# Moving the tie slots to GpSimd, the quarter sums to TensorE and half of the gap sums to VectorE, with scores and products issued earlier at both ends

## The reference, cut to what matters

```python
q = (x @ Wq.T).reshape(b, n, 2, HEADS, DIM_KEY).transpose(2, 0, 1, 3, 4)
sim = jnp.einsum('pbnhd,hkpd->pbnhk', q, keys)       # 2 x 8 vectors of 32 scores a token
sx, ix = jax.lax.top_k(sim[0], TOPK)                 # 16 best of each
sy, iy = jax.lax.top_k(sim[1], TOPK)
all_scores = (sx[..., :, None] + sy[..., None, :]).reshape(b, n, HEADS, TOPK * TOPK)
scores, pk_indices = jax.lax.top_k(all_scores, TOPK) # 16 best sums of pairs, and their places
wd = W_down[pk_indices]; wu = W_up[pk_indices]
h = gelu(jnp.einsum('bnd,bnhkd->bnhk', x, wd)) * jax.nn.softmax(scores, axis=-1)
return jnp.einsum('bnhk,bnhkd->bnd', h, wu)
```

## Time and profile before

| | |
|---|---|
| Median of 3 runs | 279.29 us (279.06 to 279.59) |
| Profiled execution, its own time | 281.1 us |
| Its span, first to last instruction | 279.4 us |
| VectorE busy | 259.9 us, 93% |
| ScalarE busy | 235.6 us, 84% |
| TensorE busy | 237.8 us, 85% |
| GpSimd busy | 226.0 us, 81% |
| Mean granted TensorE clock | 0.982 |

### The profile page before, as it was taken

The page is one execution under the profiler, slowest core; times in us unless marked ns, Lnnn a source line. Parts: engine busy times, 40 slices in busy tenths (PEclk is TensorE's granted clock), DMA queues, the critical chain, the costliest instruction groups (busy, mean ns, idle before and its releaser), DMA issues.

```text
span 279.4 us, 7039 instructions
## 1 busy us (share of the span) xinstructions
PE 237.8 (85%) x1562; PEld 176.8 (63%) x1562; DVE 259.9 (93%) x1715; ACT 235.6 (84%) x1048; POOL 226.0 (81%) x344
## 2 busy tenths in 40 slices
PE   7899689797889888978898889888988898879891
PEld 7456243575577667766776577657765776568690
DVE  5899999969999999999999999999999999995885
ACT  2554766868989999899999999999999999996853
POOL 7889701447688899989898989898989898989672
PEclk9999999979999999999999999999999999997997
DMA  7920000000000000010001000100010001000102
GB/s 179 279 74 1 2 0 0 2 1 0 5 0 0 5 0 1 13 31 0 2 3 40 1 0 5 39 0 5 0 39 4 1 0 41 1 1 4 38 1 77
DMA packets 11228, 6.23 MB, mean 22 GB/s; under 512 B 1457, under 2 KB 10674, under 8 KB 11186
## 3 DMA queue, kind: packets, MB, share of 16 engines
q1 hardware_dynamic: 9858, 5.12, 6.9%
q10 hardware_dynamic: 1328, 0.66, 1.1%
HBM read 3.67 MB, written 2.10 MB: 21 GB/s over the span
## 4 chain that ended last, share of the span: by engine, by line
PE 32%; ACT 32%; POOL 19%; issue 13%; DVE 3%; POOLq 0%; ACTq 0%; DVEq 0%
ACT prob L837 6%; PE scratch L1640 4%; PE sim L1548 4%; ACT p_win L936 3%; POOL past L485 3%; POOL squareT L500 3%; ACT gap L759 3%; PE t_bank L1566 3%; ACT away L971 3%; PE s_bank L1742 3%; PE s_bank L1736 2%; ACT spare L856 2%; PE s_bank L1531 2%; ACT sideT L747 2%; ACT side L729 2%
## 5 line engine op out<-in xcount | busy, mean ns | idle before, releaser
L1194 DVE MAX8 top<-rest 128x8 f32<-128x40 f32 x512 | 57.2, 184 | 0.1
L1144 DVE MAX8 top<-sim 128x8 f32<-128x32 f32 x496 | 54.0, 181 | 2.0 <-PE sim L1548 1.9
L837 ACT ACTIVATE prob<-drop 128x50 f32<-128x50 f32 x224 | 51.5, 255 | 0.0
L837 ACT ACTIVATION_READ_ACCUMULATOR prob<-drop 128x1 f32 x224 | 47.1, 212 | 0.0
L500 POOL TENSOR_TENSOR squareT<-sideT 100x512 bf16<-100x512 bf16 x31 | 32.3, 1041 | 6.7 <-ACT sideT L747 6.6
L513 POOL TENSOR_TENSOR wgt<-prob,rden 128x400 f32<-128x400 f32 x30 | 25.7, 855 | 11.8 <-DVE rden L1136 11.7
L1548 PE MATMUL sim<-sim_w,xT_all 128*128 128x512 f32 x64 | 34.7, 625 | 0.5 <-ACT xT_all L784 0.5
L485 POOL TENSOR_TENSOR past<-gap,last 128x400 f32<-128x400 f32 x31 | 26.8, 863 | 9.8 <-DVE last L1218 9.8
L507 POOL TENSOR_TENSOR drop<-gap,out_by 128x400 f32<-128x400 f32 x30 | 31.0, 1033 | 1.1 <-ACT out_by L736 1.1
L1566 PE MATMUL t_bank<-gaps_of,topT 128*128 128x200 f32 x128 | 29.2, 352 | 1.7 <-ACT topT L752 1.7
L1218 DVE MAX8 last<-slot_gap 128x8 f32<-128x22 f32 x256 | 24.4, 168 | 1.1
(11 more groups left out here) (295 smaller groups left out, 753.1 us busy)
## 6 DMA issues: line engine op xcount, KB each, us to landing
out<-y_sb SPq DMA_DIRECT2D x7, 256.0 KB, 2.3
x_sb<-in_L_attn_hidden_states SPq DMA_DIRECT2D x2, 256.0 KB, 4.0
fwq_sb<-in_L_ffn_Wq ACTq DMA_DIRECT2D x2, 256.0 KB, 5.8
x_sb<-in_L_attn_hidden_states SPq DMA_DIRECT2D x1, 512.0 KB, 5.4
wc_sb<-in_L_attn_Wc SPq DMA_DIRECT2D x1, 256.0 KB
out<-last_y SPq DMA_DIRECT2D x2, 128.0 KB, 1.9
wo_in<-in_L_attn_Wo SPq DMA_DIRECT2D x1, 192.0 KB
keys_sb<-in_L_ffn_keys ACTq DMA_DIRECT2D x1, 128.0 KB, 3.4
```

The source lines that it names most:

```text
L837: last = nc.scalar.activation(prob[d][:, h, :], drop[:, h, :], ACT.Exp, scale=-1.0, accum_out=den[d][:, h:h + 1])
L1144: last = nc.vector.max(top[n % 3][:, v, 0:8], sim_bank[n % 2][:, bass.ts(v, KEYS)])
L1194: last = nc.vector.max(top[n % 3][:, v, 8:16], rest[:, v, :])
```

## The change

1. **Tie slots.** In turns 4 to 31 GpSimd makes the spare slots: new `ties_of(n)`, three dependent instructions on 128 x 128 elements, right behind `past_of(n-2)`. It waits for `sum_above(n)`, which goes first in VectorE's turn and writes a tile `counts` instead of the score bank. `next_8(n)` waits for `ties_done`. `sim_used` is now said by `strike_above`. Tiles 0 to 3 keep VectorE's two instructions.
2. **Quarters.** `add_quarters` is gone; `expert_weights` adds the four heads in PSUM with two products instead of one transpose. `wgt4` has two buffers.
3. **Gaps.** For tiles 3, 4, 7, 8, ... 27, 28 (14 tiles) ScalarE's `out_by_of` and GpSimd's `drop_of` are replaced by VectorE's `keep_gaps`, one instruction that reads `f_bank` and `gap`, in the turns with j = 2 and 3. `transpose_sides` of the next tile waits for it.
4. **The start.** The token masks are transposed before `count_places(0)`, the block product of row 0 before the sides of tile 1, `scores(5)` before the pairs, and row 0's window scores before turn 4 instead of in it. `mark_above(3)` goes ahead of a gate reciprocal.
5. **The last row.** Row 7's block product moves from turn 31 to turn 30, in the place of the windows' value projection, which goes behind turn 31. In turn 31 `next_8(31)` isn't split; TensorE's `top_columns(31)`, `pair_gaps(31)` and `block_scores(7)` and ScalarE's `take_topT(31)` and `take_gaps(31)` are in the turn instead of behind it; GpSimd's `past_of(30)` goes ahead of L598, and L604 behind `drop_of(29)`. `late_gelu` goes ahead of `maxima(7)`.

```diff
+        def kept_by_vector(n):
+            return TB - 1 <= n < TILES - 3 and n % TB in (0, TB - 1)
...
             def drop_of(n):
-                pool.wait_ge(out_by_done, n + 1)
+                if kept_by_vector(n):
+                    return
+                pool.wait_ge(out_by_done, out_bys_until(n))
...
-            def add_quarters(n):
-                pool.wait_ge(wgt4_done, n + 1)
-                nc.gpsimd.tensor_tensor(wgt2[n % 2][:, :, :], wgt4[:, 0:2, :], wgt4[:, 2:4, :],
-                                        ALU.add).then_inc(wgt2_done, 1)
...
+            def ties_of(n):
+                pool.wait_ge(summed_above, n + 1)
+                pool.wait_ge(top_done, 2 * n)
+                nc.gpsimd.tensor_tensor(tie[:, :, :], counts[:, :].unsqueeze(2).to_broadcast([P, VECS, 8]),
+                                        tie_rank[:, :].unsqueeze(1).to_broadcast([P, VECS, 8]),
+                                        ALU.subtract).then_inc(tie_step, 1)
+                pool.wait_ge(tie_step, 2 * (n - TB) + 1)
+                nc.gpsimd.tensor_scalar(tie_off[:, :, :], tie[:, :, :], SPILL, 0.0, ALU.mult, ALU.min
+                                        ).then_inc(tie_step, 1)
+                pool.wait_ge(tie_step, 2 * (n - TB) + 2)
+                nc.gpsimd.tensor_tensor(rest[:, :, KEYS:KEYS + 8], tie_off[:, :, :],
+                                        top[n % 3][:, :, 7:8].to_broadcast([P, VECS, 8]),
+                                        ALU.add).then_inc(ties_done, 1)
...
                 if j == 0:
                     past_of(n - 2)
+                    ties_of(n)
                     drop_of(n - 3)
                     weigh(n - 4)
                     add_halves(n - 4)
-                    add_quarters(n - 4)
                     square_of(n - 2)
...
-                                               ALU.mult, ALU.add).then_inc(struck, 1)
+                                               ALU.mult, ALU.add).then_inc(sim_used, 1)
             def sum_above(n):
-                dve.wait_ge(struck, n + 1)
-                nc.vector.tensor_reduce(sim_bank[n % 2][:, 0:TIES], above[:, :, :], AX_X, ALU.add
-                                        ).then_inc(summed_above, 1)
+                dve.wait_ge(above_done, n + 1)
+                if n >= 1:
+                    dve.wait_ge(ties_done, n)
+                nc.vector.tensor_reduce(counts[:, :], above[:, :, :], AX_X, ALU.add).then_inc(summed_above, 1)
...
             def next_8(n, h):
                 dve.wait_ge(sim_used, n + 1)
+                dve.wait_ge(ties_done, n + 1)
...
+            def keep_gaps(n):
+                dve.wait_ge(count_ready, n + 1)
+                dve.wait_ge(gap_out, n + 1)
+                dve.wait_ge(prob_done, n)
+                nc.vector.scalar_tensor_tensor(drop[:, :, :].rearrange("p h c -> p (h c)"),
+                                               f_bank[:, 0:HEADS * CANDS], OUT_SCALE,
+                                               gap[n % 4][:, :, :].rearrange("p h c -> p (h c)"),
+                                               ALU.mult, ALU.max).then_inc(drop_done, 1)
...
             def turn(n):
                 b, j = divmod(n, TB)
+                sum_above(n)
                 strike_above(n)
                 if n + 1 in tiles:
                     first_8(n + 1, [0])
-                sum_above(n)
                 if j == 0:
                     maxima(b - 1)
                 invert_sums(n - 4)
-                spill_above(n)
+                if kept_by_vector(n - 3):
+                    keep_gaps(n - 3)
                 if n + 1 in tiles:
                     first_8(n + 1, [1])
-                put_ties(n)
-                if n + 1 in tiles:
                     mark_above(n + 1)
                 next_8(n, 0)
+                if n == TILES - 1:
+                    next_8(n, 1)
                 gaps_of_pairs(n - 1)
...
-                if n < TILES - TB:
-                    pe.wait_ge(wgt2_done, n + 1)
-                    last = nc.tensor.transpose(o, wgt2[n % 2][:, :, :].rearrange("p h c -> p (h c)"), ident[:, :])
+                if n <= TILES - TB:
+                    pe.wait_ge(wgt4_done, n + 1)
+                    w, heads = wgt4[n % 2], HEADS // 2
...
+                    project_pairs(b)
+                    expert_weights(n - 4)
+                    top_columns(n)
+                    window_scores(b)
+                    pair_gaps(n)
+                    block_scores(b)
                     count_places(n - 2)
...
             pair_gaps(2)
-            count_places(0)
             transpose_masks()
             project_window(0, U_VW, wv_sb)
+            count_places(0)
             count_ranks()
+            project_blocks(0, range(RATIO))
             transpose_sides(1)
-            project_blocks(0)
             project_selected(0)
+            scores(5)
+            project_pairs(0)
             count_places(1)
-            project_pairs(0)
-            scores(5)
+            window_scores(0)
```

More of the change, by code:

```diff
@@ L235, in program @@
         wgt = [sb(f"wgt{i}", [P, HEADS, CANDS]) for i in range(2)]
-        wgt4 = sb("wgt4", [P, HEADS // 2, CANDS])
-        wgt2 = [sb(f"wgt2_{i}", [P, 2, CANDS]) for i in range(2)]
+        wgt4 = [sb(f"wgt4_{i}", [P, HEADS // 2, CANDS]) for i in range(2)]
         last_drop = [sb(f"last_drop{i}", [P, HEADS, CANDS]) for i in range(2)]
@@ L334, in summed, with out_bys_until @@
             return n >= TILES - 4
+        def kept_by_vector(n):
+            return TB - 1 <= n < TILES - 3 and n % TB in (0, TB - 1)
+        def out_bys_until(n):
+            return sum(not kept_by_vector(m) for m in range(n + 1))
         def sums_until(n):
@@ L623, in turn @@
                     add_halves(n - 4)
-                    add_quarters(n - 4)
                     square_of(n - 2)
                 elif j == 2:
+                    past_of(n - 2)
+                    ties_of(n)
                     if b >= 2:
                         gate_silu(b - 2)
-                    past_of(n - 2)
                     weigh(n - 4)
@@ L643, in turn @@
                     square_of(n - 2)
-                    add_quarters(n - 4)
-                    if b >= 2 and n < TILES - 1:
+                    if b >= 2:
                         add_input(b - 2)
+                else:
+                    past_of(n - 2)
+                    ties_of(n)
+                    weigh(n - 4)
+                    add_halves(n - 4)
+                    drop_of(n - 3)
+                    square_of(n - 2)
+                    past_of(n - 1)
+                    gate_attention(b - 2)
             count_matrix()
@@ L659, in _ @@
                 turn(n)
-            past_of(TILES - 2)
+            drop_of(TILES - 3)
             add_input(B - 3)
-            drop_of(TILES - 3)
             square_of(TILES - 2)
@@ L1783, in turn @@
                     pair_gaps(n - 1)
-                    project_window(b, U_VW, wv_sb)
+                    if b < B - 1:
+                        project_window(b, U_VW, wv_sb)
+                    else:
+                        project_blocks(b, range(RATIO))
                     if n + 2 in tiles:
@@ L1788, in turn @@
                     count_places(n - 2)
+                elif n < TILES - 1:
+                    top_columns(n - 1)
+                    project_selected(b)
+                    pair_gaps(n - 1)
+                    transpose_sides(n - 2)
+                    project_blocks(b, range(RATIO))
+                    scores(n + 2)
+                    project_pairs(b)
+                    count_places(n - 2)
+                    expert_weights(n - 4)
                 else:
```

123 lines of the change are left out of this document (67 added, 56 removed).

## The result

The changed kernel takes 292.85 us (median of 4 runs, 292.08 to 294.96), the kernel before 279.44 in the same session (279.06 to 279.95). The ratio is 1.047, 95% interval 1.0435 to 1.0512: 4.7% slower, where 278.0 was predicted and the range ended at 281.8. The medians are 13.4 us apart; the profiled executions span 290.3 and 279.4 us, 10.9 apart.

The account below looks back on a forecast made before the run. The prediction took the steady part as a balance in which GpSimd becomes the bound. Start -2.85, five steady rows +2.4 and tail -0.85 gave -1.3 us: 278.0 us from 279.29, range 274.8 to 281.8.

Parts of the forecast that it names:

- The start: Turns 4 to 8: waits in turn 4 vanish, turn 5 starts 2.0 us sooner, `next_8(9)` 2.85 us sooner.
- rival 3: Start: it gives nothing lasting, as ScalarE or slow TensorE products hold the gain; 279.3 us, no change; chance 0.14.
- TensorE gets four more products ...; hidden: TensorE, steady rows: four more products of some 0.3 us, hidden as it has 24.61 of 28.17 us busy.
- the forecast's 28.65: Steady row: GpSimd's summed work of 28.65 us becomes the bound, against 28.17 now, +0.48 a row.
- The price of the ties: GpSimd's three `ties_of` instructions: 1.37 us a turn, bounds 1.31 and 1.57; 5.48 for four turns.
- rival 1: GpSimd's `ties_of` from turn 8: small instructions cost more than their size says, 1.57 a turn, 282.4 us; chance 0.28.
- GpSimd's sum without waits: GpSimd, steady row: its 1.30 us of waits go, since factors are always there, leaving only its work, 28.65.
- a loop through ScalarE and TensorE that I have left out: Sign against the forecast: GpSimd waiting for another engine in a steady row longer than 28.8 us.
- Who waits for the ties: `next_8`, and VectorE's turn behind it, waits about 1 us for GpSimd once a row, with j = 1 alone.
- The tail: Last row and after: maxima at about 258.0 instead of 258.96, last exponentials about 1.3 us sooner; gives 0.85 us.

Follow-up runs that it names:

- e11: e6 with the quarters on GpSimd again, leaving only the orders of start and tail; 278.04 us, 0.9918 of the kernel before.
- e6: The changed kernel with all tie slots back on VectorE in the score bank (PSUM) and without `keep_gaps`; 280.41 us, 1.0015 of the kernel before.
- e5: The changed kernel with all tie slots back on VectorE in the score bank (PSUM), `keep_gaps` staying; 281.50 us, 1.0057 of the kernel before.
- e2: The changed kernel without the middle of GpSimd's three tie instructions, a step left out of the result; 282.16 us, 1.0098 of the kernel before.
- e9: The changed kernel with TensorE's `expert_weights` and `count_places` moved behind the first half of `attention_out`; 288.15 us, 1.0303 of the kernel before.
- e10: e6 with the tie slots of the turns with j = 1 on GpSimd; 288.66 us, 1.0300 of the kernel before.
- e1: The changed kernel with all tie slots back on VectorE, their tiles still in SBUF; 305.79 us, 1.0859 of the kernel before.
- e13: e6 with the tie slots of the turns with j = 2 on GpSimd; 283.91 us, 1.0154 of the kernel before.
- e15: The changed kernel with the middle tie instruction as a product with a constant 0, comparison left out of the result; 289.17 us, 1.0320 of the kernel before.
- e8: The changed kernel with the middle tie instruction's two scalars from an SBUF column instead of immediates; 299.25 us, 1.0648 of the kernel before.

## Why the prediction was wrong

- **The start**: right in what moves, not in what it is worth. The maxima of turn 4 came 2.67 sooner, `sim` was no wait, and turn 5 begins at 66.41 in e11 for 68.58, 2.17 sooner (2.0 forecast). But the sum took its holes, 1.86 and 0.67 in turn 4 and 3.11 before the last maxima, from an execution whose clock had fallen just there. It also set its span (279.4) equal to the median of others (279.29), where its own time was 281.1. The forecast went on to 2.85 by `next_8(9)`; the changed kernel had 1.08 left at turn 8's maxima. The runs place part of the difference: e11 has 2.02 there (first maxima at 88.59), e6, which differs by the quarters, 1.33 (89.28). By its sign (turn 5 no sooner than 67.5) rival 3 is out, and e11 shows that the orders gain something that lasts: 1.5 to 1.9 at like clocks, start and tail together, where 2.85 + 0.85 = 3.7 was forecast. That products run slowly in turn 4, which rival 3 names, is what the clock row shows.
- **"TensorE gets four more products ...; hidden"**: the step that failed quietly. TensorE's 24.61 of 28.17 busy was no cover, since those of the turn with j = 1 (0.44 us for 0.11) lie in the one stretch that the loop runs through. 0.43 a row, 28.61 against 28.18 (e6, e11). It doesn't show in the changed kernel's sum, because there GpSimd is longer, but rows of 28.57 to 28.64 (e5, e6, e2) are what is left when GpSimd is relieved and the quarters stay: in e2 cheaper ties brought the row to the forecast's 28.65 and no further.
- **The price of the ties**: mis-sized, 1.37 taken, 1.60 measured (0.40, 0.64 and 0.42 with their gaps), just above the upper bound of 1.57. It was L463 where L472 with 0.536 was the safer neighbour. +0.92 a row. This is rival 1, and alone it would have given about 282 to 283.
- **GpSimd's sum without waits**: the step that failed most. The other terms of 28.65 were right: 28.65 + 0.92 = 29.57, and e9's row, in which GpSimd waits for nothing, is 29.61. But in the changed kernel the row is 29.57 + 0.87 of wait = 30.44, measured 30.47. The prediction had costed the ties as work on one engine, and named "a loop through ScalarE and TensorE that I have left out" as what would prove it wrong. The loop is what happened: the ties stand ahead of the halves, the halves hold TensorE's queue, and the queue holds `sideT`. The wait that the earlier trace rows show there before, 0.24 for `sideT`, was its sign, and I read it as slack.
- **Who waits for the ties**: right. `next_8` waits for them 0.43 us in the turn with j = 1 alone (1 us forecast). The larger waits of VectorE in a row, 1.45 for its maxima and 1.02 for `slot_gap`, are the loop's.
- **The tail**: right as an order, wrong in this kernel. In e11 the last row is 26.04 against 27.44 before, 1.40 shorter (0.85 forecast for the whole tail), but the 27.44 have a clock fall in them, which cost about 1.5 us in the long row of e10; so the gain of this order isn't shown by itself; in the changed kernel the unsplit `next_8(31)` waits 1.60 for GpSimd and the last row is 28.56. Behind the maxima e11 gains 0.31 (275.7 - 255.57 against 279.4 - 258.96), as the forecast's 1.3 - 0.96 has it. One loss there was left out: VectorE's `past` of the tail, both inputs in SBUF, takes 0.57 us before and 1.62 in the changed kernel (1.63 in e11), where GpSimd works beside it without a gap; in the kernel before GpSimd stands still beside it (2.25 of wait). That this is the contention of e1 is argued, not tested.

The account of the row: 28.17 + 0.48 (forecast) + 0.92 (price) + 0.87 (loop) = 30.44. The account of the profiled spans, which missed by 10.9 + 1.3 = 12.2: the start 2.85 - 1.08 = 1.77, the five rows 11.09 - 2.4 = 8.69, the tail 0.89 + 0.85 = 1.74. Against the medians the miss is 13.4 + 1.3 = 14.7; of the 2.5 between, 1.7 is by how much the profiled execution of the kernel before, with its clock falls in turn 4 and the last row, lies above its median (281.1 against 279.4), and 0.8 by how much the changed kernel's lies below (292.1 against 292.9).

Open: how the 1.5 to 1.9 us of e11 divide between start and tail, and what makes TensorE's clock fall in some runs and not in others. Whether a cheaper form of the ties would pay on e11 wasn't tried.

## What to carry to other kernels

An engine's work and its waits don't add up alone: before giving work to an engine with slack, follow each thing it produces to the next in-order queue, and ask what that queue holds behind it; the price is what the work exceeds the cover at that place (0.70 reckoned, 0.67 measured in e13), not what it exceeds the engine's idle share. Here four busy engines with waits of 0.2 to 0.5 us each were one loop, and products added in its path cost their full length where no wait stood behind them (0.33 in j = 1) and 0.10 of 0.37 where one did (j = 3). Before a hole in a profile goes into a sum, read the granted clock beside it and compare the profiled execution's own time with the median: here 281.1 against 279.3. And where a scratch tile lies can decide more than which engine works on it: VectorE's ties cost about 22 us more with their tiles in SBUF (302.6 and 304.4, the two runs of e1 that its ratio counts) than in PSUM (281.5, e5), twice the 11.4 that it cost to give them to GpSimd.

## What the hardware showed that was not expected

- A VectorE instruction with both inputs in SBUF, 0.27 us when GpSimd pauses, took 1.76 and 1.02 beside GpSimd's back-to-back work and ended 0.15 after it (e1); over 32 of each form the means were 0.77 and 0.67. With one input in PSUM they were 0.29 and 0.27 (before and e5).
- TensorE's granted clock fell to half for some 3 to 4 us (0.50 in the kernel before from 58 to 60 us, 0.54 in e10 from 130 to 132). It fell within some 2 us behind a wait of TensorE (0.59 and 1.06 us before, 0.55 in e10), and the same waits stand in rows without a fall. Two score products took 1.92 us for 1.08, and a row of e10 1.5 us more.
- On GpSimd, 128 elements in 16 groups of 8 cost 0.40 to 0.46 as a tensor and tensor instruction, 0.64 as `mult` and `min` with two immediates, 0.80 with the two scalars from a column (the changed kernel, e15, e8).
